# Causal attention in chunks of 512 queries and steps of four heads instead of head by head

## The chip, the cores and the metric

The program runs on one core of a Trainium2 chip. Its five engines (PE is TensorE, DVE is VectorE, ACT is ScalarE, POOL is GpSimd, SP only issues DMAs) run instruction streams of their own and meet at semaphores. The metric is the time of one execution on the device in microseconds. Before the change three runs took 2035.68 to 2046.28, median 2041.61.

## The reference, cut to what matters

A batch of one, 2048 tokens of width 128, goes through eight layers: Mamba with a feed-forward, a mixture of experts, attention, the mixture again, a second Mamba, a low-rank MLP, attention with ALiBi, the MLP again. Only the two attentions are changed. Each is, after one or two layer norms,

```python
q, k, v = split(x @ W)                    # 16 heads of 8
s = q @ k.T                               # (q is scaled by 8 ** -0.5)
s = s + slope[head] * (key - query)       # the second attention only (ALiBi)
s = where(key > query, -inf, s)           # causal
x = x + softmax(s) @ v @ W_out
```

It is to be exact to about float32, so q and k are each split into three bfloat16 parts, and a score is one matmul over 72 rows (3 x 3 x 8; 84 with ALiBi).

## The kernel before, in words

The function is `attention`, called twice (tags a0 and a1). Tokens fall into 16 tiles of 128 and into four chunks of 512 (`NC`). All of it goes by score tiles, of which a head has 40, in two forms:

- **q-items** (`item`, L1641 and L1807) compute scores with queries on partitions, in a tile of 128 queries by up to 512 keys, only to find each query's maximum. PE writes four groups of 32 rows into a PSUM bank of `ps_q` (three banks), and DVE reduces it (L1817) or, on the diagonal, masks and reduces it (L1814).
- **k-items** (`scores`, L1658) compute the scores again with keys on partitions, 128 keys by up to 512 queries, with three more rows that subtract the maxima. ACT takes the exponential (L1757) into `probs`, and `times_v` (L1675) multiplies four items at a time by v in float32, with a column of ones that gives the sums. The four 32-row groups of PE work side by side into `ps_o`; ACT copies the result of a chunk to `o_sb` (L1763).

Between them stand the maxima of a head: DVE negates them (L1822), POOL splits them into three bfloat16 parts (`split_maxima`, L1892), PE turns them (`turn`, L1632), DVE copies them out (L1805) and SP moves them by DMA into the operand (`load_maxima`, L1961). The k-items of the head wait for that.

The order is by head: head 0's 40 q-items, then 14 more (`LEAD`), and from then on one q-item per k-item. Inside a head chunk follows chunk, each with more keys (4, 8, 12 and 16 items). On PE, `scores` runs three items ahead of `times_v`; the streams of all engines are in order.

Operands: the parts of q and k go chunk by chunk to DRAM (`store_parts`, L1936), since each of their rows has to be repeated, and come back as `q_op` and `k_op` with 2048 columns, one pair per head, four pairs in turn (`load`, L1957; two DMAs, four with ALiBi). POOL copies v of a head next to the ones (`place`, L1887). SP's order in a head: stores of `o_sb` (`store`, L1966, four DMAs per chunk to DRAM), the maxima of the next head, the outputs of the head before back from DRAM with heads on partitions (`load_output`, L1972), the operands four heads on.

The output can only be made when all heads are there. For each chunk: DVE adds the four row groups of the sums and inverts them (`invert`), PE spreads them over the partitions (`spread`, L1692), DVE and POOL add the four groups of the outputs (`add_partials`, L1835, POOL's half L1931), DVE divides, PE multiplies by W_out (`output`), DVE adds to x and begins the next layer norm. Chunks 0 and 1 have their PE parts placed inside the last head's stream (L1730 to L1738); chunks 2 and 3 follow it. These parts use two PSUM tensors of their own, in the place of the projections'.

## Time and profile before

| | |
|---|---|
| median of 3 runs | 2041.61 us |
| the profiled execution | 2046.62 us |
| its span, first to last instruction | 2044.8 us |
| busy in the span | PE 89%, DVE 78%, ACT 57%, POOL 27% |
| mean granted TensorE clock | 0.943 |
| first attention | 508.0 to 986.0 us |
| second attention | about 1508 to 1985 us |

Busy shares are means over layers of quite different kinds, so they say little of the attentions: a stretch of the trace, cut out by its times, says more. "Granted clock" is the share of full speed that the TensorE throttle gave, 1.0 for 2.4 GHz and 0.5 for 1.2 GHz. A row of a timeline has the start in microseconds from the span's start, the duration, the engine, the line, what is written and read, how many instructions are merged (x), and in brackets the idle time of the engine before it and what ended that. SPq and ACTq rows are DMA issues; their duration is the issue's, not the transfer's.

### The profile page before, as it was taken

What the parts mean: (1) busy time and instruction counts of PE and PEld (TensorE: products, weight loads), DVE (VectorE), ACT (ScalarE), POOL (GpSimd) and SP (SyncE); (2) the same over time, 40 slices, a digit from 0 to 9 for tenths busy, and PEclk for the clock granted to TensorE, in tenths of its full rate; (3) what the DMA queues carried; (4) which work ended last, traced back from release to release, by engine and by line L of the source; (5) the groups of instructions that cost most, each with busy time, mean ns of one, the idle gap of its engine ahead of it and who ended that gap; (6) DMA issues with size and microseconds to landing.
All of it is one profiled execution on the core that took longest, in us unless ns stands there. A gap on an engine that the chain in (4) does not pass through costs nothing. (4 is left out here: it accounts for less than half of the span.)

```text
span 2044.8 us, 47996 instructions
## 1 busy us (share of the span) xinstructions
PE 1824.5 (89%) x18588; PEld 980.9 (48%) x18588; DVE 1587.9 (78%) x3383; ACT 1174.7 (57%) x2361; POOL 555.7 (27%) x520
## 2 busy tenths in 40 slices
PE   6888888999799999997899978888869999999967
PEld 2444454444255555554544434443634555555454
DVE  7899965666889999983465579999668999999545
ACT  4775623122278888885322256765443888888815
POOL 3898920000200000001000049988230000000022
PEclk9999998999699999998799989999886999999969
DMA  5343300310312222211041114443021233322200
GB/s 169 122 134 123 119 1 4 87 51 27 109 34 54 55 52 51 49 27 22 1 84 51 31 58 119 129 119 103 1 73 51 54 56 60 57 57 41 31 4 21
DMA packets 68527, 127.30 MB, mean 62 GB/s; under 512 B 20679, under 2 KB 30932, under 8 KB 66828
## 3 DMA queue, kind: packets, MB, share of 16 engines
q1 hardware_dynamic: 67884, 123.70, 24.2%
q8 instruction: 147, 2.41, 0.5%
q14 instruction: 80, 0.66, 0.1%
q10 hardware_dynamic: 416, 0.54, 0.1%
HBM read 105.58 MB, written 16.84 MB: 60 GB/s over the span
## 5 line engine op out<-in xcount | busy, mean ns | idle before, releaser
L1757 ACT ACTIVATE a_probs<-a_ps_k 128x512 f32<-128x512 f32 (+3 forms) x1280 | 598.6, 547 | 225.6 <-PE a_ps_k L1671 129.7
L1653 PE MATMUL a_ps_q<-a_k_op,a_q_op 84*32 84x512 bf16 (+7 forms) x5120 | 536.3, 366 | 25.4 <-DMA a_k_op<-a_k_parts 10.1
L1817 DVE TENSOR_REDUCE a_maxes<-a_ps_q 128x1 f32<-128x512 f32 x768 | 504.2, 686 | 67.8 <-PE a_ps_q L1653 65.2
L1667 PE MATMUL a_ps_k<-a_q_op,a_k_op 87*32 87x512 bf16 (+7 forms) x5120 | 517.8, 353 | 2.4 <-ACT a_probs L1757 0.8
L1689 PE MATMUL a_ps_o<-a_probs,a_vh 128*32 128x512 f32 (+3 forms) x2752 | 319.2, 509 | 0.8 <-ACT a_probs L1757 0.8
L1653 PEld LDWEIGHTS a_ps_q<-a_k_op,a_q_op 72*32 72x32 bf16 (+1 forms) x5120 | 186.9, 97 | 172.2 <-DVE a_maxes L1817 69.2
L1814 DVE CUSTOM_DVE_ANT_0 a_ps_q<-a_ps_q,all_c_mask_q 128x128 f32<-128x128 f32 (+3 forms) x512 | 248.2, 496 | 4.7 <-PE a_ps_q L1653 3.7
L1667 PEld LDWEIGHTS a_ps_k<-a_q_op,a_k_op 75*32 75x32 bf16 (+1 forms) x5120 | 184.9, 96 | 136.2 <-ACT a_probs L1757 85.6
L1088 ACT ACTIVATE e_silu<-e_psg,all_me_b 128x512 f32<-128x512 f32 x128 | 87.7, 687 | 229.0 <-PE e_psg L1020 228.9
L1897 POOL CAST a_max_parts<-a_neg_max 128x16 bf16<-128x16 f32 x32 | 6.3, 197 | 751.5 <-DVE a_neg_max L1822 751.5
L1171 DVE SCALAR_TENSOR_TENSOR e_mid<-e_psv,all_me_b,e_silu 128x512 f32<-128x512 f32 x128 | 95.7, 749 | 132.0 <-PE e_psv L1022 128.0
L172 POOL TENSOR_TENSOR all_rstd<-all_var_eps,all_c_minus_half 128x4 f32<-128x4 f32 x36 | 36.8, 1023 | 504.4 <-DVE all_var_eps L161 504.4
L662 POOL TENSOR_TENSOR m0st_read<-m0st_state,m0st_c_rows 128x1024 f32<-128x1024 f32 x64 | 149.6, 2358 | 12.4 <-DVE m0st_state L590 6.4
L590 DVE TENSOR_TENSOR_SCAN m0st_state<-m0st_decay,m0st_carry,m0st_drive 128x1024 f32<-128x1024 f32 x64 | 146.8, 2334 | 7.6 <-DVE m0st_drive L570 6.4
L590 DVE TENSOR_TENSOR_SCAN m1st_state<-m1st_decay,m1st_carry,m1st_drive 128x1024 f32<-128x1024 f32 x64 | 146.8, 2334 | 7.2 <-DVE m1st_drive L570 6.1
L662 POOL TENSOR_TENSOR m1st_read<-m1st_state,m1st_c_rows 128x1024 f32<-128x1024 f32 x64 | 149.5, 2357 | 9.9 <-PE m1st_psy L414 5.8
L1671 PE MATMUL a_ps_k<-all_c_mask_k,all_c_ident_b 128*32 128x128 bf16 x2048 | 149.3, 221 | 0.7 <-issue 0.7
L1020 PE MATMUL e_psg<-e_xT,all_me_w_T 128*128 128x512 f32 x256 | 134.7, 608 | 1.5 <-ACT e_xT L197 1.5
L1022 PE MATMUL e_psv<-e_xT,all_me_w_T 128*128 128x512 f32 x256 | 133.2, 602 | 0.0
L1009 PE MATMUL e_pso<-e_hid,all_me_w_T 128*128 128x512 f32 x256 | 119.0, 594 | 5.0 <-DVE e_hid L1180 5.0
L1689 PEld LDWEIGHTS a_ps_o<-a_probs,a_vh 128*32 128x32 f32 x2752 | 106.7, 110 | 26.7 <-issue 2.1
L414 PE MATMUL m0st_psy<-m0st_read,all_c_ident 128*128 128x512 f32 x256 | 115.8, 594 | 1.9 <-POOL m0st_read L662 1.8
(295 smaller groups left out, 2582.8 us busy)
## 6 DMA issues: line engine op xcount, KB each, us to landing
m0st_c_rows<-m_bc_rows SPq DMA_DIRECT2D x32, 512.0 KB
e_w_rows<-e_comb SPq DMA_DIRECT2D x64, 256.0 KB, 3.2
m1st_c_rows<-m_bc_rows SPq DMA_DIRECT2D x32, 512.0 KB
a_q_op<-a_q_parts SPq DMA_DIRECT2D x30, 288.0 KB
a_k_op<-a_k_parts SPq DMA_DIRECT2D x30, 288.0 KB
a_outputs<-a_o_sb SPq DMA_DIRECT2D x480, 18.0 KB
m0st_b_rows<-m_bc_rows SPq DMA_DIRECT2D x32, 256.0 KB
m1st_b_rows<-m_bc_rows SPq DMA_DIRECT2D x32, 256.0 KB
```

Source lines behind the costliest of these rows:

```text
L590: dve.tensor_tensor_scan(state[half(q, h)][:, :], decay[half(q, h)][:, :], drive[:, h, :], carry[:, h, q % NS:q % NS + 1], ALU.mult, ALU.a ...
L662: pool.tensor_tensor(read[h][:, :], state[half(q, h)][:, :], c_rows[q % 2][:, :], ALU.mult).then_inc(read_ready, 1)
L1009: pe.matmul(pso[:, :], w["w3_T"][:, e, f, :], hid[:, k % SL, :], start=k == 0, stop=k == K - 1, skip_group_check=True).then_inc(hid_free, 1)
L1020: pe.matmul(psg[:, f, :], w["w1_T"][:, e, fs], xT[:, tokens(c)], start=True, stop=True).then_inc(g_ready, 1)
L1022: pe.matmul(psv[:, f, :], w["w2_T"][:, e, fs], xT[:, tokens(c)], start=True, stop=True).then_inc(v_ready, 1)
L1653: last = pe.matmul(ps_q[32 * r:32 * r + 32, use % QB, 0:width], q_op[h % SLOT][0:NR, part(t, r)], k_op[h % SLOT][0:NR, kc * CH:kc * CH + w ...
L1667: last = pe.matmul(ps_k[32 * r:32 * r + 32, b % KB, 0:width], k_op[h % SLOT][:, part(j, r)], q_op[h % SLOT][:, c * CH + first:c * CH + fir ...
L1671: last = pe.matmul(ps_k[32 * r:32 * r + 32, b % KB, 0:P], g["ident_b"][:, part(0, r)], g["mask_k"][:, :], start=False, stop=True, skip_gro ...
L1689: pe.matmul(ps_o[rows, c % 2, lo:hi], vh[h % SLOT][:, j, :], probs[:, a % PSLOT, lo - first:hi - first], start=j < 4, stop=j >= TPC * c, s ...
L1757: act.activation(probs[:, n % PSLOT, 0:width], ps_k[:, b % KB, 0:width], ACT.Exp).then_inc(exp_done, 1)
L1814: dve.tensor_tensor_reduce(bank, bank, g["mask_q"][:, CH - width:CH], 1.0, -3e38, ALU.add, ALU.max, found).then_inc(q_read, 1)
L1817: dve.tensor_reduce(found, bank, AX.X, ALU.max).then_inc(q_read, 1)
```

## The change

The loops are turned round. A step is now one chunk of queries for four heads, and a call has 16 steps: chunk 0 for heads 0 to 3, 4 to 7, 8 to 11, 12 to 15, then chunk 1, and so on. A step of chunk 0 has 16 items, of chunk 1 32, of chunk 2 48, of chunk 3 64. The number and the shapes of all items stay as they were.

- q-items run one step and 14 items ahead (`position`): while a step's k-items run, the q-items of the next step are spread evenly over them, two per k-item in step 3, 1.5 in step 7, 1.33 in step 11.
- Maxima are turned per step (16 columns, as before per head).
- `q_op` holds a step (four buffers); keys are kept in `k_op`, one tensor per chunk, for all heads, and are loaded once. SP issues for each step, three steps on, one DMA for q and one for k per head, eight in all (nine with ALiBi), with 512 columns each instead of 2048.
- v stands in one tensor `vh` with the ones beside it, written by the projections; POOL's copy per head goes.
- A store moves two heads, and is issued twice a step. A chunk's outputs come back in five DMAs (chunk 3's by step, the last step's straight from `o_sb`).
- The outputs of chunks 0 to 2 are made inside the stream of the next chunk, at fixed positions (`prepare_at` to `normalise_at`); PE's parts use banks of `ps_q`. POOL adds sums and outputs there (`add_partials`); for chunk 3 DVE does most of it.
- Operands now share memory with the parts, so exponentials begin after all parts are stored.

The core of the diff:

```diff
+        HG = 4
+        GROUPS = HEADS // HG
+        STEPS = NC * GROUPS
+        turn_at = {begin[s + 1] + TURN: s for s in range(STEPS)}
+        POSITIONS = NI + TURN + 1
+        def position(b):
+            s, i = k_items[b][0], b - begin[k_items[b][0]]
+            after = size[s + 1] if s < LAST else size[s]
+            return min(begin[s + 1] + LEAD + -(-(i + 1) * after // size[s]), POSITIONS)
+        def event(c, n):
+            return position(begin[GROUPS * (c + 1)] + n)
+        prepare_at = {event(c, 24): c for c in range(NC - 1)}
+        spread_at = {event(c, 34): c for c in range(NC - 1)}
+        output_at = {event(c, 42): c for c in range(NC - 1)}
+        stats_at = {event(c, 46): c for c in range(NC - 1)}
+        normalise_at = {event(c, 60): c for c in range(NC - 1)}
...
@@ tensor
+            for b in range(NI):
+                if b + KB < NI:
+                    scores(b + KB)
+                first_forms(done, position(b))
+                done = position(b)
+                if b % 4 == 3:
+                    times_v(b - 3)
+            spread(NC - 1)
+            output(NC - 1)
...
@@ scalar
+            for c in range(1, NC):
+                act.wait_ge(stored[c], STORED)
...
@@ gpsimd
+            def add_partials(c):
+                add_sums(c)
+                add_upper(c)
+                if c:
+                    pool.wait_ge(q_ready, output_use[c - 1] + 1)
+                pool.tensor_tensor(total[:, :], oT[:, 0, :], oT[:, 1, :], ALU.add).then_inc(lower_ready, 1)
+                pool.wait_ge(lower_ready, c + 1)
+                pool.wait_ge(upper_ready, c + 1)
+                pool.tensor_tensor(total[:, :], total[:, :], upper[:, :], ALU.add).then_inc(total_ready, 1)
+            for s in range(STEPS):
+                c = chunk_of(s) - 1
+                if c > 0 and s % GROUPS == 1:
+                    add_partials(c)
+                split_maxima(s)
+                if c >= 0 and s % GROUPS == 1:
+                    if c == 0:
+                        add_partials(c)
+                    ahead.power(pool, c)
...
@@ sync
+            def load(s):
+                c, h = chunk_of(s), head(s, 0)
+                if s % GROUPS == 0:
+                    sp.wait_ge(stored[c], STORED)
+                if s >= SLOT:
+                    sp.wait_ge(k_ready, begin[s - SLOT + 1])
+                for hh in range(HG):
+                    loaded = step_loaded[s % SLOT] if s else first_head[hh]
+                    q_rows = q_dram[c, h + hh, :, :, :].rearrange("a d t -> (a d) t").unsqueeze(1)
+                    sp.dma_start(q_op[s % SLOT][0:PAIRS, hh * CH:(hh + 1) * CH],
+                                 q_rows.broadcast_to([SPL * DH, SPL, CH])).then_inc(loaded, 16)
+                    parts_k = k_dram[c, h + hh:h + hh + 1, :, :, :].rearrange("o d b t -> o (d b) t")
+                    sp.dma_start(k_op[c][0:PAIRS, (h + hh) * CH:(h + hh + 1) * CH],
+                                 parts_k.broadcast_to([SPL, DH * SPL, CH])).then_inc(loaded, 16)
...
+            load_k_rows(0)
+            store_parts(0)
+            for s in range(SLOT - 1):
+                load(s)
+                store_parts(s + 1)
+            for c in range(1, NC - 1):
+                load_k_rows(c)
+            load_maxima(0)
+            for c in range(1, NC):
+                sp.wait_ge(stored[c], STORED)
+            for s in range(STEPS):
+                c = chunk_of(s)
+                if s:
+                    store(s - 1, 1)
+                if s + SLOT - 1 < STEPS:
+                    load(s + SLOT - 1)
+                if s == GROUPS:
+                    load_k_rows(NC - 1)
+                if c == 0:
+                    load_maxima(s + 1)
+                if c and s % GROUPS == 0:
+                    load_outputs(c - 1, s - 1, 0, HEADS)
+                if c == NC - 1 and s % GROUPS:
+                    load_outputs(c, s - 1, head(s - 1, 0), HG)
+                if s < LAST:
+                    store(s, 0)
+                    if c:
+                        load_maxima(s + 1)
+            for hh in range(HG):
+                sp.wait_ge(o_read, HG * LAST + hh + 1)
+                if hh < HG - 1:
+                    move_sums(sp, hh)
+                move_outputs(sp, hh)
```

## Rows read from the trace of the kernel before

**Rows 1.** Busy time by stretch (from:to, length, busy us and count per engine).

```profile
core 0: us, PE busy (x) PEld busy (x) DVE busy (x) ACT busy (x) POOL busy (x), PEclk, DMA share, GB/s
508.00:559.30 51.30, 39.34 (x294) 15.10 (x298) 43.58 (x121) 12.85 (x22) 12.46 (x24) 0.69 0.36 109
602.30:626.70 24.40, 24.16 (x485) 14.19 (x475) 22.45 (x59) 20.22 (x45) 1.04 (x5) 1.00 0.29 52
928.00:944.50 16.50, 15.21 (x245) 6.07 (x237) 0.00 (x0) 15.86 (x36) 0.00 (x0) 1.00 0.33 43
944.50:963.60 19.10, 13.19 (x110) 8.40 (x111) 8.34 (x22) 4.09 (x9) 3.98 (x3) 0.73 0.05 8
963.60:986.00 22.40, 13.44 (x66) 11.88 (x66) 14.09 (x46) 0.60 (x1) 5.25 (x4) 0.59 0.02 3
```

**Rows 2.** Waits between 920 and 965 (total us, times, longest).

```profile
DVE a0ou_pair L1827 <- DMA a_sums<-a_outputs: 21.4, 1, 21.4
PE a0ou_ps_s L1697 <- DVE a0ou_inv L1833: 6.0, 2, 5.0
```

**Rows 3.** Timeline of PE in a head's middle (start, duration, ...).

```profile
583.54 1.03 PE L1689 MATMUL a_ps_o<-a_probs,a_vh 128*32 128x512 f32 x8
584.40 0.23 PE L1667 MATMUL a_ps_k<-a_q_op,a_k_op 75*32 75x128 bf16 x4
584.46 0.23 PE L1671 MATMUL a_ps_k<-all_c_mask_k,all_c_ident_b 128*32 128x128 bf16 x4
584.52 0.39 PE L1653 MATMUL a_ps_q<-a_k_op,a_q_op 72*32 72x512 bf16 x4
584.74 0.39 PE L1667 MATMUL a_ps_k<-a_q_op,a_k_op 75*32 75x512 bf16 x4
```

**Rows 4.** Timeline of DVE there.

```profile
582.60 0.69 DVE L1817 TENSOR_REDUCE a_maxes<-a_ps_q 128x1 f32<-128x512 f32 x1 [0.64 <-PE a_ps_q L1653]
583.21 0.42 DVE L1814 CUSTOM_DVE_ANT_0 a_ps_q<-a_ps_q,all_c_mask_q 128x256 f32<-128x256 f32 x1
583.55 0.68 DVE L1817 TENSOR_REDUCE a_maxes<-a_ps_q 128x1 f32<-128x512 f32 x1
```

**Rows 5.** DMA issues of SP in the timeline, and one line's durations (ns).

```profile
517.33 0.58 SPq L1942 DMA_DIRECT2D a_k_parts<-a0pr_k_parts  x1
...
522.15 0.90 SPq L1949 DMA_DIRECT2D a_q_op<-a_q_parts  x1
...
535.09 0.78 SPq L1949 DMA_DIRECT2D a_q_op<-a_q_parts  x1
535.91 0.71 SPq L1950 DMA_DIRECT2D a_k_op<-a_k_parts  x1
...
581.72 0.76 SPq L1963 DMA_DIRECT2D a_q_op<-a_max_T  x1
...
938.93 1.33 SPq L1979 DMA_DIRECT2D a_sums<-a_outputs  x4
...
L1970 SPq DMA_DIRECT2D a_outputs<-a_o_sb x480: 264/315/2105, 566.1 to 1930.1; - x160
```

**Rows 6.** Timeline of ACT in the last head.

```profile
936.65 3.27 ACT L1757 ACTIVATE a_probs<-a_ps_k 128x512 f32<-128x512 f32 x7
```

**Rows 7.** Timeline of the call's end, PE and ACT's DMA queue.

```profile
960.98 2.00 PE L1697 MATMUL a0ou_ps_s<-a0ou_inv,all_c_sel_head 128*128 128x64 f32 x16 [0.97 <-DVE a0ou_inv L1833]
...
964.37 1.16 PE L1705 MATMUL a0ou_ps_y<-all_a_wo,a0ou_total 128*128 128x128 f32 x8
...
965.25 3.60 ACTq L1605 DMA_DIRECT2D a_sums<-a_o_sb  x4
```

**Rows 8.** Timeline of the adds, DVE and POOL.

```profile
946.67 1.36 POOL L1931 TENSOR_TENSOR a0ou_upper<-a_oT 128x512 f32<-128x512 f32 x1 [22.56 <-DMA a_sums<-a_outputs]
946.95 1.17 DVE L1831 TENSOR_TENSOR a0ou_inv<-a0ou_pair 128x64 f32<-128x64 f32 x1
...
967.88 0.22 DVE L1831 TENSOR_TENSOR a0ou_inv<-a0ou_pair 128x64 f32<-128x64 f32 x1
```

More of the change, by code:

```diff
@@ L1464, in attention @@
         QB = 3
+        PB = 3
         LEAD = 14
         TURN = 5
[L1467 removed]
+        THIRD = 6
         JT = CH // SB
@@ L1583, in attention @@
-        USES = len(item_use) + len(turn_use)
-        def stream(turn, item, first, last):
-            for p in range(first, min(last, POSITIONS)):
-                if turned_at(p) is not None:
-                    turn(turned_at(p))
-                if p < NQ * HEADS:
-                    item(p // NQ, p % NQ)
-        def pieces(n):
-            c, j, first, width = k_items[n]
+        LOADS = 16 * (2 * HG + (1 if alibi else 0))
+        KROWS = [16 * (3 if alibi else 1)] + [16 * (2 if alibi else 1)] * (NC - 1)
@@ L1595, in pieces, with chunk_of, head @@
+        spread_use[NC - 1], output_use[NC - 1] = uses, uses + 1
+        def chunk_of(s):
+            return s // GROUPS
+        def head(s, hh):
+            return HG * (s % GROUPS) + hh
+        def pieces(b):
+            s, hh, j, first, width = k_items[b]
+            c = chunk_of(s)
             if c and j == TPC * c:
@@ L1656, in item, with spread @@
                 last.then_inc(q_ready, 1)
-            def scores(b):
-                h, n = divmod(b, NK)
-                c, j, first, width = k_items[n]
-                if n == 0:
-                    pe.wait_ge(max_loaded[h % SLOT], 16 * (h // SLOT + 1))
+            def spread(c):
+                use = spread_use[c]
+                pe.wait_ge(inverted, c + 1)
+                bank_free(use)
+                for j in range(SB):
+                    last = pe.matmul(ps_q[:, use % QB, j * JT:(j + 1) * JT], g["sel_head"][:, j, :], inv[:, :], start=True, stop=True)
+                last.then_inc(q_ready, 1)
@@ new lines, in output, with first_forms @@
+            def output(c):
+                use = output_use[c]
+                pe.wait_ge(q_read, spread_use[c] + 1)
+                bank_free(use)
+                for j in range(TPC):
+                    last = pe.matmul(ps_q[:, use % QB, tile(j)], total[:, tile(j)], w["wo"][:, :], start=True, stop=True)
+                last.then_inc(q_ready, 1)
+            def first_forms(begins, stops):
+                for p in range(begins, stops):
+                    if p in turn_at:
+                        turn(turn_at[p])
+                    if p in spread_at:
+                        spread(spread_at[p])
+                    if p in output_at:
+                        output(output_at[p])
+                    if p < NI:
+                        item(p)
@@ L1714, in _ @@
             pe.wait_ge(max_set, 3)
-            stream(turn, item, 0, NQ + LEAD)
-            pe.wait_ge(ones_loaded, 16 * SLOT)
+            pe.wait_ge(norm.copied, NC)
+            for bank in range(2):
+                for r in range(4):
+                    pe.matmul(ps_o[32 * r:32 * r + 32, bank, :], zeros[:, :], g["sel"][:, 0:4, :], start=True, stop=True,
+                              skip_group_check=True)
+            first_forms(0, begin[1] + LEAD)
             pe.wait_ge(v_copied, NC)
+            pe.wait_ge(v_set, 1)
             for o in range(2):
@@ L1721, in _ @@
                 scores(b)
[L1722 to L1741 removed]
+            done = begin[1] + LEAD
+            for b in range(NI):
[7 more added lines that the diff above has]
+            output(NC - 1)
         @block.scalar
@@ L1867, in _ @@
                 remove_first(c)
-            third_of_k(NC - 1)
             dve.wait_ge(max_set, 3)
-            stream(turn, item, 0, POSITIONS)
-            dve.wait_ge(k_ready, NK * LAST)
-            dve.wait_ge(o_back, 16 * BACKS * LAST)
-            for c in range(NC):
-                invert(c)
-                add_partials(c)
-                divide(c)
-                if c:
-                    ahead.normalise(dve, c - 1)
-                add(c)
-                if c + 1 < NC:
-                    dve.wait_ge(added, c + 1)
-                    ahead.stats(dve, c)
+            for p in range(POSITIONS):
+                if p == THIRD:
+                    third_of_k(NC - 1)
+                if p in prepare_at:
+                    invert(prepare_at[p])
+                if p in turn_at:
+                    turn(turn_at[p])
+                if p in spread_at:
+                    divide(spread_at[p])
+                if p in output_at:
+                    add(output_at[p])
+                if p in stats_at:
+                    ahead.stats(dve, stats_at[p])
+                if p in normalise_at:
+                    ahead.normalise(dve, normalise_at[p])
+                if p < NI:
+                    item(p)
```

507 lines of the change are left out of this document (220 added, 287 removed).

## The prediction

> **What bounds the kernel now.** I read the page's slices first: the two attention calls fill slices 11 to 19 and 31 to 39 of 40, with TensorE at nine tenths in most. Both run the changed function, so the case is this function, twice. I then cut the first call (508.0 to 986.0) into stretches [rows 1]. Until 559.3, the first exponential, the projections and the first 54 q-items run, at a granted clock of 0.69. One head in the middle takes 24.40 us with PE busy 24.16, DVE 22.45 and ACT 20.22, at full clock. From 928.0 the last head's k-items run alone, ACT busy 15.86 of 16.50. From 944.5 to 963.6 PE, ACT and DVE are all partly empty; from 963.6 to 986.0 chunks 2 and 3 of the output are made one after the other. So PE bounds the body with DVE close behind, and the edges cost 51.3 us ahead of the first exponential and 22.4 behind the last.
>
> The waits of the tail [rows 2] name the hole before 963.6: DVE waits 21.4 us for `a_sums`, and PE for `a_inv`. PE's stream asks for the sums of chunks 0 and 1 in the middle of the last head, before they are back. The 9 tiles left at 944.5 take 19 us where ACT needs about 0.5 each: some 14.5 us are lost.
>
> **Durations.** Four 32-row matmuls of 512 columns hold PE 0.22, of 128 columns or masks 0.06 (by their starts, [rows 3]), so a thousand columns cost 0.42 us at full clock. P times V of four full tiles holds it 0.86; for four diagonal tiles I take 0.64 by their 384 columns, and 0.85 plus 0.16 of zero fills in chunk 0. A reduce holds DVE 0.60, a masked reduce of 256 columns 0.34 [rows 4]; 128, 384 and 512 then take 0.21, 0.47 and 0.60, together 1.62. PE per head and chunk: chunk 0 2.29, chunk 1 (7168 columns, PV 1.49) 4.48, chunk 2 7.04, chunk 3 9.6; sum 23.4 against 24.40 measured. I put 3% on top, not the measured 4%, since long and short tiles stand less unevenly beside each other. A step of four heads: 9.4, 18.5, 29.0, 39.7. DVE for a step's q-items, with 0.5 for turn and negation: 7.3 in chunk 0 (diagonal tiles alone follow one another more slowly), then 16.6, 26.2, 35.8.
>
> **Ahead of the first exponential.** Before, the first load was issued at 522.15, behind the parts of chunk 1 [rows 5]. Now it goes right behind the parts of chunk 0, at about 521, so the first q-item comes 2 us earlier. But SP now issues eight loads a step: 0.78 and 0.71 with gaps, 1.58 a head, 6.35 a step [rows 5]. Its order is load 0, parts 1 (four DMAs near 0.6, 2.4), load 1, parts 2, load 2, parts 3, then the maxima: 521 + 3 x (6.35 + 2.4) + 0.6 + 0.76 = 548.6, landed 2.3 later. (The maxima issued at 581.72 for 0.76 served scores at 584.74 [rows 5, 3]: 2.3 is an upper end.) Only 30 narrow q-items are needed first, not 54, and they are done by about 545: SP ends this stretch. First exponential at 551.5 instead of 559.3: 7.8 gained. Ends: 10 if landings are quicker, 5 if they are as slow as that of the parts (issued 517.33, used by 522.15).
>
> **Steps 0 to 2.** Here I expect the largest loss in the body. In a short step SP issues, in this order, the second store (it waits for the fourth head's output of the step before), eight loads, the maxima. Queued behind its wait are the loads and the maxima; for the maxima PE's scores of the next step wait, and behind those PE's q-items too, as its queue is in order, and then DVE. From the first scores of a step: last PV and copy with hand-overs 3.3, four stores of 0.32 [rows 5] 1.3, loads 6.35, maxima 0.76, landing 2.3: 14.0 us, against 9.4 of PE work. Step 0 starts at the lower clock and takes 10, its maxima being ahead. So 10 + 14 + 14 = 38. Ends: 30 if everything of SP is hidden, 46 if PE works at 1.2 GHz besides.
>
> **The body.** The q-items run one step ahead and so meet a longer step at 3, 7 and 11, where DVE bounds: 16.6, 26.2, 35.8, not PE's 13, 22, 32.5. There the maxima also have fewer positions in which to land (nine at up to double rate, less three tiles): 1.6 + 0.9 + 0.5. Steps 4 to 6: 55.5; 8 to 10: 87.0; 12 to 14: 119.1 less 1.9 for 13 tiles without q-items. Step 15 is ACT's: seven full tiles take 3.27 [rows 6], a diagonal group 1.41 and a copy 0.47 by the same rate, so 12 x 0.477 + 1.41 + 0.47 = 7.6 a head, 30.4. Three tiles at the seam add 1.8, the end takes 1.3 off: 1.8 + 16.6 + 3.0 + 55.5 + 26.2 + 87.0 + 35.8 + 117.2 + 30.4 - 1.3 = 372.2.
>
> The outputs of chunks 0 to 2 now stand in this stream: spread 2.00 and product 1.16 on PE [rows 7], 3 x 3.16 = 9.5. On DVE some 4.4 a chunk are added: the 14.09 it had for two chunks and the end of a third [rows 1] make 6, less the adds that go to GpSimd. PE and DVE overlap but for 0.3 a chunk: 10.5. Ends: 3 if they fall in gaps, 15 if they never overlap. DVE's reciprocal waits for sums that went to DRAM and back and for GpSimd's two adds; its divide for three more, 1.36 each beside work [rows 8]; every q-item of DVE is queued behind, and PE waits for DVE to free a bank. The chunk's loads are issued 12 to 15 us into the step, the waits stand at 17 and 23. I take 4 us in all; ends 0 and 15. Sum: 38 + 372.2 + 10.5 + 4 = 424.7, against 404.3 from 559.3 to 963.6 before: 20.4 lost, although the 14.5 us hole is gone. What takes them: 78 tiles at the end without q-items instead of 54, DVE-bound seams, outputs in the stream, SP.
>
> GpSimd's adds beside DVE have a price in the trace: DVE's two-input add for `a_inv` took 1.17 beside GpSimd's `a_upper`, 0.22 alone [rows 8]. A q-item reads at most its mask from SBUF, and 22.45 of 24.40 us of DVE are q-items; I price nothing, the end is 5 us a chunk if they block each other throughout. The Trainium skill (SBUF — State Buffer, "Who interferes with whom") says that DVE with two SBUF inputs contends with GpSimd's reads, a reduce never. By that rule the price is 0; the row agrees for the two-input case.
>
> **The end.** Only chunk 3 is left. From the last exponential: PV and copy to 965.25 1.7, four DMAs on ACT's queue 3.60 [rows 7], landing 2.2, sums and reciprocal 1.2, spread 4.0 and product 2.3 at the lower clock (twice rows 7), divide and add 1.5: 16.5 instead of 22.4, so 5.9 gained. Ends 3 and 9.
>
> **Sum.** Per call -7.8 + 20.4 - 5.9 = +6.7, twice +13.4 (the second call's slices look the same). The profiled execution took 2046.6 (span 2044.8), 5 above the median of 2041.6; 13.4 on the median gives **2055**.
>
> **Rivals.** (1) Not slower: the even mix hides more. A head of 24.40 holds 23.4 of columns. If the long steps run 1% above their columns, outputs fall in gaps, round trips are early and SP's chain is 2 us shorter in each of two steps, a call loses 5 + 7 + 4 + 4 = 20 less: 2055 - 40 = 2015. For it: in a head where PE bounds, DVE still idles 0.64 at a time before a reduce [rows 4], so imbalance costs. Against: PE is 99% busy. It decides once a step of chunk 3 takes under 39 us and steps 1 and 2 under 12. (2) Clock: SP's holes of 4.6 us leave PE idle, and over the hole before 963.6 the granted clock was 0.73 [rows 1]. PE's work of steps 0 to 3 at 1.2 GHz is 2 x (3 x 9.4 + 13) = 82 instead of 54.6: +27 a call, 2109; half of it 2082. The Trainium skill (TensorE: Matmul & The Clock Gate, "HAM oscillation — how this bites in real kernels") tells of kernels that pay this at each DMA wait; the trace agrees in so far as the clock fell at the hole. (3) The sums' round trip: issued by 940.26, used at 946.67 [rows 5, 8], 6.4 us. Then each of three chunks waits 5 us at reciprocal and divide: +11 a call, 2077. (4) The hole only moves: the last chunk's own sums are as late, 22.4 stays behind the last exponential: 2067.
>
> **Chances.** Forecast 0.50 (own range 2040 to 2068), rival 1 0.22, rival 2 0.11, rivals 3 and 4 0.17. "No change" is within 0.5%, 10 us, about what a measurement of this kernel can tell. Faster 0.24 (rival 1 and an edge of the forecast), same 0.28 (the forecast's lower half), slower 0.48. The range leaves out half of rival 1 and half of rival 2: 2022 to 2084.
>
> **What would show it.** First exponential 43 to 44 us into a call; steps 1 and 2 near 14 us each, PE idle for the maxima's DMA while SP issues without a gap; DVE over 95% busy in steps 3, 7 and 11; the last step ACT-bound near 30; 16.5 us behind the last exponential. The forecast is wrong if the maxima never hold PE up, if a long step takes under 39 us, or if DVE waits 5 us or more for sums.

## The result, and the profile after

The changed kernel takes 2123.36 us (median of 4 runs, 2118.36 to 2128.21), the kernel before 2042.97 beside it: a ratio of 1.0396, 95% interval 1.0368 to 1.0423. It is 80 us slower where 13 were forecast, and outside the range. The profiled execution took 2124.45, its span is 2122.4.

The first call now runs from 508.0 to 1023.9, 37.9 us longer; the second is 44.3 longer, and the rest of the program is 4.6 shorter between the two profiles. The loss stands between the first and the last exponential of a call: 451.6 and 452.2 us where it was 404.3 and 403.0. Behind the last exponential 15.4 and 15.6 are left of 22.4 and 23.8. Cut at the first exponential of each step, as [rows 1] were cut (from:to, length, busy us by engine, granted clock, DMA share, GB/s), the page after reads:

```profile
508.00:556.90 48.90, 26.53 (x218) 13.22 (x218) 28.52 (x103) 12.74 (x22) 10.40 (x15) 0.69 0.37 112
568.60:583.60 15.00, 9.24 (x229) 7.52 (x224) 8.16 (x36) 7.81 (x21) 0.80 (x4) 0.93 0.27 66
583.60:599.80 16.20, 12.35 (x246) 10.00 (x242) 9.15 (x28) 8.14 (x21) 0.80 (x4) 0.82 0.24 57
599.80:619.70 19.90, 16.62 (x290) 11.15 (x286) 16.36 (x46) 8.72 (x20) 0.80 (x4) 0.86 0.18 44
619.70:644.70 25.00, 20.47 (x415) 11.78 (x411) 19.61 (x55) 16.46 (x36) 2.87 (x8) 0.96 0.38 91
644.70:670.30 25.60, 24.86 (x426) 13.81 (x422) 20.18 (x61) 16.79 (x36) 4.29 (x7) 0.90 0.16 38
670.30:690.20 19.90, 19.55 (x400) 11.23 (x394) 18.96 (x53) 16.38 (x36) 0.80 (x4) 1.00 0.20 48
690.20:717.20 27.00, 25.04 (x458) 11.12 (x454) 26.36 (x66) 17.05 (x36) 0.80 (x4) 1.00 0.15 36
782.00:811.70 29.70, 29.49 (x562) 16.68 (x558) 27.51 (x66) 24.34 (x53) 0.80 (x4) 1.00 0.14 33
811.70:849.80 38.10, 36.33 (x618) 14.98 (x614) 36.46 (x82) 25.68 (x52) 0.80 (x4) 1.00 0.11 26
849.80:895.60 45.80, 44.41 (x750) 22.74 (x746) 40.36 (x96) 33.33 (x69) 6.32 (x10) 1.00 0.21 48
895.60:936.40 40.80, 40.52 (x722) 20.08 (x718) 38.09 (x87) 32.91 (x69) 0.80 (x4) 1.00 0.08 17
974.90:1008.50 33.60, 31.15 (x452) 10.91 (x448) 0.00 (x0) 31.70 (x69) 0.00 (x0) 1.00 0.10 21
1008.50:1023.90 15.40, 6.59 (x34) 5.57 (x34) 4.22 (x7) 0.60 (x1) 1.26 (x1) 0.60 0.03 6
```

These are steps 1 to 7, 10 to 13 and 15 between the prelude and the end; 8, 9 and 14 took 33.8, 31.0 and 38.5, step 0 11.7. PE's work is unchanged, so read length against PE busy first: steps 1 to 4 have 3 to 6 us without PE. Then read the clock: it is under 1.00 in the same steps and in 5. There PE is busy 24.86 us against 19.55 in step 6; some 3.2 of the difference are the output's spread and product [rows 7], and at full clock the same step took 23.1 instead of 25.6 (experiment 4). From step 6 on the clock is full; long beside their neighbours are the steps with an output (8, 9, 12), those whose q-items are of the next chunk (7, 11) and ACT's last step.

The waits of PE over the whole program (total, times, longest) name what ends the holes; in the kernel before PE never waited for the maxima's DMA in its first call:

```profile
PE a_ps_k L1723 <- DMA a_q_op<-a_max_T: 50.1, 12, 13.8
PE a_ps_q L1689 <- DVE a_inv L1869: 14.6, 2, 7.3
```

One hole closely, first SP's queue in step 1 (four stores, four pairs of loads of which the last stands here, the maxima), then PE's timeline, then the stretch of the hole and the one behind it:

```profile
570.98 1.36 SPq L2031 DMA_DIRECT2D a_outputs<-a_o_sb  x4
572.44 0.81 SPq L2013 DMA_DIRECT2D a_q_op<-a_q_parts  x1
...
578.04 0.71 SPq L2016 DMA_DIRECT2D a_k_op<-a_k_parts  x1
578.79 0.73 SPq L2024 DMA_DIRECT2D a_q_op<-a_max_T  x1
```

```profile
582.84 0.62 PE L1723 MATMUL a_ps_k<-a_q_op,a_k_op 75*32 75x512 bf16 x4 [5.44 <-DMA a_q_op<-a_max_T]
```

```profile
577.40:582.80 5.40, 0.00 (x1) 0.00 (x0) 0.62 (x2) 0.77 (x2) 0.00 (x0) 0.87 0.34 94
582.80:588.20 5.40, 5.36 (x81) 4.16 (x85) 2.12 (x8) 2.49 (x6) 0.00 (x0) 0.50 0.02 4
```

SP issues without a gap and reaches the maxima at 578.79, just as forecast; they land 3.3 us after their issue ends, not 2.3 (in the second call it is 2.4 here and 2.1 a step later). And when PE comes back its clock is 0.50, half of 2.4 GHz. The Trainium skill (TensorE: Matmul & The Clock Gate, "HAM oscillation — how this bites in real kernels") describes this pair, a wait for a DMA and then work at half clock, once per wait; the trace agrees three times in the first call.

Step 4 shows the same with another transfer ahead. The last output step's traffic on SP (sums, the 1 MB of partial outputs, stores, maxima), and the answer on PE:

```profile
632.42 3.37 SPq L2042 DMA_DIRECT2D a_sums<-a_outputs  x4
635.83 0.60 SPq L2044 DMA_DIRECT2D a_oT<-a_outputs  x1
636.48 1.87 SPq L2031 DMA_DIRECT2D a_outputs<-a_o_sb  x4
638.39 0.80 SPq L2024 DMA_DIRECT2D a_q_op<-a_max_T  x1
...
644.05 0.62 PE L1723 MATMUL a_ps_k<-a_q_op,a_k_op 75*32 75x512 bf16 x4 [3.96 <-DMA a_q_op<-a_max_T]
```

Here landing takes 4.9 us. In the second call the same step fails in another way: the sums come late, GpSimd adds them late, DVE waits to invert, and PE behind it (DVE's timeline and the waits of 1675 to 1683):

```profile
1679.86 0.55 DVE L1869 RECIPROCAL a_inv<-a_inv 128x64 f32<-128x64 f32 x1 [4.56 <-POOL a_inv L1949]
...
PE a_ps_q L1680 <- DVE a_maxes L1856: 4.4, 1, 4.4
```

### The profile page after: what moved, and what is told of

Same layout as the page of the kernel before. It is cut to its first block and busy times, and to the rows that moved or that the text cites. A ratio compares the mean times of both kernels' runs of the same rounds, so it can differ in the third digit from the quotient of the medians.

```text
span 2122.4 us, 47829 instructions
## 1 busy us (share of the span) xinstructions
PE 1839.6 (87%) x18604; PEld 955.4 (45%) x18604; DVE 1579.5 (74%) x3359; ACT 1185.8 (56%) x2361; POOL 562.0 (26%) x498
## 5 line engine op out<-in xcount | busy, mean ns | idle before, releaser
L1792 ACT ACTIVATE a_probs<-a_ps_k 128x512 f32<-128x512 f32 (+3 forms) x1280 | 608.3, 544 | 247.2 <-PE a_ps_k L1727 139.2
L1723 PE MATMUL a_ps_k<-a_q_op,a_k_op 75*32 75x512 bf16 (+7 forms) x5120 | 536.3, 357 | 57.7 <-DMA a_q_op<-a_max_T 50.1
L1680 PE MATMUL a_ps_q<-a_k_op,a_q_op 72*32 72x512 bf16 (+7 forms) x5120 | 527.9, 363 | 45.9 <-DVE a_maxes L1856 13.8
L1745 PE MATMUL a_ps_o<-a_probs,a_vh 128*9 128x512 f32 (+3 forms) x2752 | 322.4, 511 | 0.9 <-ACT a_probs L1792 0.9
L1727 PE MATMUL a_ps_k<-all_c_mask_k,all_c_ident_b 128*32 128x128 bf16 x2048 | 162.1, 227 | 0.0
L414 PE MATMUL m1st_psy<-m1st_read,all_c_ident 128*128 128x512 f32 x256 | 116.1, 594 | 2.0 <-POOL m1st_read L662 1.7
```

What stands on the lines that cost most here:

```text
L414: last = pe.matmul(psy[:, h, chunk(b)], g["ident"][:, :], read[h][:, chunk(b)], start=False, stop=q % NS == NS - 1, skip_group_check=True)
L1680: last = pe.matmul(ps_q[32 * r:32 * r + 32, use % QB, 0:width], q_op[s % SLOT][0:NR, tokens:tokens + 32], k_op[kc][0:NR, h * CH:h * CH + w ...
L1723: last = pe.matmul(ps_k[32 * r:32 * r + 32, b % KB, 0:width], k_op[j // TPC][:, keys:keys + 32], q_op[s % SLOT][:, hh * CH + first:hh * CH ...
L1727: last = pe.matmul(ps_k[32 * r:32 * r + 32, b % KB, 0:P], g["ident_b"][:, 32 * r:32 * r + 32], g["mask_k"][:, :], start=False, stop=True, ...
L1745: pe.matmul(ps_o[32 * r:32 * r + DH + 1, bank, lo:hi], vh[:, HEADS * j + h, :], probs[:, a % PSLOT, lo - first:hi - first], start=j < 4, s ...
L1792: act.activation(probs[:, b % PSLOT, 0:width], ps_k[:, b % KB, 0:width], ACT.Exp).then_inc(exp_done, 1)
```

## The experiments

Theories: **T1**, the maxima's way through SP's queue (issue order, landing behind other DMAs, half clock behind each hole); **T2**, the outputs of chunks 0 to 2 inside the stream; **T3**, the step structure itself, where it loads DVE. Gains below are differences between the changed kernel's ratio, 1.0396, and the ratio of the experiment, each with the kernel before beside it, times 2040 us; by the two intervals such a gain is known to 6 to 10 us. "Body" below is the stretch from the first to the last exponential of a call in the profiled execution, 451.6 and 452.2 us in the kernel after; it leaves out what varies in the other layers.

**1. Maxima ahead of the loads.**

```diff
-                load(s + 3); load_maxima(s + 1)        # step order of SP
+                store(s, 0); load_maxima(s + 1); load(s + 3)
```

> SP issues the next step's maxima ahead of the loads of the step after the next three (and load 2 of the prelude behind the first maxima); nothing else changes. Theory T1 (most of the 80 us is PE waiting for the maxima, 50.1 us in the trace after, because SP issues them behind eight loads of 0.7 to 0.8 us and they land behind these, and because PE's clock is half for 6.8 us after each hole): first exponential 4 to 5 us earlier in each call, steps 1, 2, 4 and 5 together 11 us shorter, a few us elsewhere; the waits for the maxima fall from 50.1 to under 15 us and the time to 2085 (2078 to 2095). Theory T2 (the outputs of chunks 0 to 2 in the stream cost 5 us each and more): this order changes little, the maxima wait moves behind another, 2110 to 2123. Theory T3 (the steps themselves are longer: seams where DVE bounds, a longer end without q-items): holes go, but PE then waits for DVE instead, at least 2110.

Measured 2117.56, ratio 1.0385 (1.0354 to 1.0416): 2 us, no gain beyond the noise and far from the 38 that T1 expected. The first exponential stands at 545.9 instead of 556.9, but in this profile the call itself begins 4.1 us earlier: it came 6.9 us sooner, 7.5 in the second call. Against that steps 1 and 2 grew to 18.5 and 20.1, and the body was 453.0 and 455.8. Waits of PE from 508 to 617:

```profile
PE a_ps_q L1680 <- DMA a_k_op<-a_k_parts: 16.4, 5, 6.7
PE a_ps_k L1723 <- DMA a_q_op<-a_max_T: 10.9, 5, 2.7
```

The wait moved: q-items run 30 items ahead of their k-items in steps of 16, so the loads are as urgent as the maxima, and one queue cannot put both first. T1's remedy failed, not yet T1. With nothing ahead of them the maxima landed 1.51 to 1.56 us after their issue ended (eight times).

**2. The maxima on GpSimd's queue**, SP's order as in the kernel after.

```diff
                 split_maxima(s)
+                pool.wait_ge(q_read, turn_use[s] + 1)
+                pool.dma_start(q_op[s % SLOT][NR:NR_MAX, :]..., max_T[:, :]).then_inc(max_loaded[s % SLOT], 16)
```

> SP's order stays as in the kernel after, but the maxima go out on GpSimd's own queue as soon as DVE has copied them. T1 in its form that SP's order and queue hold the maxima back: the holes of 5.44, 3.78 and 3.96 us shrink to under 1.5, 2085 (2078 to 2095), as with the other order. T1 in its form that the transfers of the loads fill the DMA engines whatever the queue: the maxima are issued 3 to 9 us earlier but take 5 to 6 us to land, so about half is gained: 2100 to 2112. T2 or T3: 2110 to 2123. The prelude's hole of 9.46 us should go to 4 or less in the first form, as there the maxima could be issued at about 543 instead of 547.94.

Measured 2101.79, ratio 1.0314 (1.0290 to 1.0337): 17 us. Steps 1 and 2 (and step 3):

```profile
559.60:569.00 9.40, 9.08 (x246) 7.93 (x240) 8.07 (x36) 7.63 (x21) 1.41 (x5) 1.00 0.27 62
569.00:580.10 11.10, 9.76 (x244) 8.01 (x236) 8.87 (x29) 7.82 (x22) 1.41 (x5) 1.00 0.36 94
580.10:599.00 18.90, 14.08 (x290) 9.00 (x281) 16.04 (x47) 8.38 (x22) 1.41 (x5) 1.00 0.27 66
```

Step 1 at 9.40 is the columns' own 9.4: SP's queue was the loss there, 10.7 us in two steps of the first call. Little of that is left at the end: the body is only 2.2 and 2.9 us shorter, since steps 4, 5, 7, 8 and 11 lose some 10 us in the first call (8 alone 3.8), and most of the gain is the stretch ahead of the first exponential, 5.2 and 8.4 us. With the 1 MB in flight the maxima took 5.4 us on this queue too (issued 618.86, 0.62, used 624.92), and steps 4 and 5 were 54.4 instead of 50.6. So both forms of T1 hold: order where loads are ahead, traffic on the shared DMA engines where the 1 MB is.

**3. Two loads a step instead of eight**, the same bytes.

```diff
-                for hh in range(HG): sp.dma_start(q_op[...hh...], ...); sp.dma_start(k_op[c][...hh...], ...)
+                sp.dma_start(q_op[s % SLOT][0:PAIRS, :], ...four heads); sp.dma_start(k_op[c][...h:h + HG...], ...)
```

> The kernel after with SP's order, but the operands of a step come in two DMAs of four heads each instead of eight of one head; the same bytes (the parts of k are stored in three DMAs instead of one a chunk, which adds two issues of 0.5 to 0.6 us to each of four chunks ahead of the first exponential). T1a (SP's issue time holds the maxima back: 8 x 0.78 = 6.3 us a step): a step's chain is some 4.5 us shorter, steps 1 and 2 fall from 15.0 and 16.2 to about 11, the hole of 9.46 before the first exponential shrinks by 2 to 5 us, 2 x 14 less: 2095 (2085 to 2102). T1b (the transfers themselves, 0.6 MB a step in the same queue, hold them back): landing stays 2.7 to 4.9 us behind the issue and the holes stay, 2112 or more. The other queue gained 5.6 and 5.2 us in steps 1 and 2 by taking away both.

Measured 2106.49, ratio 1.0334 (1.0312 to 1.0356): 13 us, between the two. A load of four heads is issued as quickly as one of one head:

```profile
568.40 0.81 SPq L2020 DMA_DIRECT2D a_q_op<-a_q_parts  x1
569.25 0.72 SPq L2023 DMA_DIRECT2D a_k_op<-a_k_parts  x1
570.10 0.73 SPq L2031 DMA_DIRECT2D a_q_op<-a_max_T  x1
...
577.06 0.62 PE L1723 MATMUL a_ps_k<-a_q_op,a_k_op 75*32 75x512 bf16 x4 [3.69 <-DMA a_q_op<-a_max_T]
```

From the step's first exponential (564.6) the maxima are issued after 5.5 us instead of 10.2, but land 6.2 us later: the bytes queued ahead come first. Of 4.7 us saved at the issue 1.8 reach the step (13.2 instead of 15.0). Steps 4 and 5 of the first call gained more, 22.5 and 23.1 at a clock of 1.00: the sums and the 1 MB go out earlier too.

**4. PE kept busy through the holes**, to price the clock alone. PE's wait for a free bank of `ps_k` moves ahead of the fill with it.

```diff
+                    for n in range(FILL.get(s, 0)):      # {2: 18, 3: 14, 4: 6, 5: 14}
+                        pe.matmul(ps_k[:, b % KB, :], g["ident_b"][0:96, :], g["sel"][0:96, 0:4, :], start=True, stop=True)
                     pe.wait_ge(max_loaded[s % SLOT], ...)
```

> The kernel after with matmuls into a bank that is overwritten next, put on TensorE between the last work before a step and its wait for the maxima: 18, 14, 6 and 14 of 512 columns ahead of the scores of steps 2, 3, 4 and 5 (3.8, 2.9, 1.3 and 2.9 us at full clock). They shorten no wait. If the half clock behind each hole (6.8 us each at 581.4, 598.4, 642.8 in the first call, four stretches in the second) is an own cost on top of the hole, the clock stays at 1.0 there, the steps behind run 2 to 3.4 us shorter each: 15 to 20 us over both calls, 2105. If PE is not what bounds the short steps behind a hole (SP's chain is), nothing comes of it: 2118 to 2125. Where a hole is shorter than its matmuls, up to 2 us is lost.

Measured 2118.69, ratio 1.0394 (1.0367 to 1.0421): no difference. In the first call it did what it should: clock 1.00 in steps 1 to 4, which with step 5 took 94.5 us instead of 101.7.

```profile
568.80:583.40 14.60, 12.94 (x248) 9.03 (x245) 8.10 (x35) 7.77 (x22) 0.80 (x4) 1.00 0.26 66
583.40:598.00 14.60, 12.86 (x260) 9.51 (x256) 8.90 (x28) 7.75 (x20) 0.80 (x4) 1.00 0.26 64
```

In the second call, which among steps 1 to 5 had the full clock in step 1 only, step 4 ran into the wait for the sums instead (5.1 us, then 13.7 us at half clock) and took 32.2 instead of 27.8. So the half clock is a cost of its own, some 7 us in the first call, but this fill does not save it on the whole.

**5. No outputs of chunks 0 to 2.** Left out: their sums, divide, product, normalisation and loads.

```diff
-        prepare_at = {event(c, 24): c for c in range(NC - 1)}     # and spread_at, output_at, stats_at, normalise_at
+        prepare_at = {}
```

> Leaves out the output projection of chunks 0 to 2 with their sums, normalisation and the loads of their partial outputs; only chunk 3 gets its output. T2: the trace after shows steps 8 and 12 at 33.8 and 45.8 us against 29.7 and 40.8 without an output, and 25.0 for step 4, so some 5 us go from each of three chunks, 32 us over both calls, and with the 1 MB load gone ahead of the maxima in step 4 its hole of 3.96 us and the half clock behind it go too, 3 to 5 us a call: 2123 - 40 = 2083. T1: only the hole of step 4 goes, the rest of the outputs lies in gaps: 2110 to 2116. The waits for the maxima stay above 35 us in both.

Measured 2081.64, ratio 1.0218 (1.0197 to 1.0240): 36 us, T2 as expected. The body says more, 428.2 and 429.7: 23 us a call. Steps 4, 5, 8 and 12 without an output, against 25.00, 25.60, 33.80 and 45.80:

```profile
615.80:637.50 21.70, 21.32 (x415) 12.67 (x411) 18.88 (x54) 16.46 (x36) 0.80 (x4) 0.92 0.21 51
637.50:656.40 18.90, 18.83 (x402) 10.70 (x397) 17.70 (x51) 16.35 (x36) 0.80 (x4) 1.00 0.21 51
702.70:732.50 29.80, 29.66 (x562) 15.77 (x558) 27.61 (x68) 24.38 (x52) 0.80 (x4) 1.00 0.14 33
829.90:870.20 40.30, 40.23 (x726) 21.48 (x722) 37.47 (x84) 32.98 (x68) 0.80 (x4) 1.00 0.10 25
```

**6. The engines' work of the outputs without the round trip.** The loads of partial outputs and sums of chunks 0 to 2 are left out; both buffers are set to one once.

```diff
-                if c and s % GROUPS == 0:
-                    load_outputs(c - 1, s - 1, 0, HEADS)
+                if s == 3: pool.memset(sums, 1.0); pool.memset(oT, 1.0)      # GpSimd, in its idle time
```

> The kernel after without the loads of the partial outputs and sums of chunks 0 to 2: GpSimd sets both buffers to one once (in step 2 or 3) and all adds, the reciprocal, divide, product and normalisation run on that, as often as before. Without outputs at all 42 us went. If the round trip is what costs (sums and 1 MB behind eight loads, the maxima behind the 1 MB: holes of 3.96 and 4.41 us with half clock behind them in steps 4 and 5), most of it goes in steps 4 and 5 and little in 8 and 12: 12 to 18 us over both calls, 2107 (2103 to 2112). If it were all round trip: 2085. If it is engines' work alone: 2118 or more. What stays of the 42 us is the work on PE and DVE, which the forecast put at 10.5 us a call.

Measured 2101.15, ratio 1.0302 (1.0285 to 1.0318): 19 of the 36 us, slightly more than expected. The body is 442.6 and 441.5, 9.0 and 10.7 shorter, more than half of it in steps 4 and 5 (21.8 and 23.2 in the first call, from 25.0 and 25.6; 20.3 and 23.2 in the second, from 27.8 and 25.2), and one us each in 8 and 12. Steps 4, 5 and 8 here:

```profile
619.60:641.40 21.80, 21.42 (x415) 12.84 (x407) 18.96 (x55) 16.46 (x37) 5.29 (x9) 0.92 0.20 50
641.40:664.60 23.20, 22.47 (x426) 13.06 (x422) 20.34 (x63) 16.43 (x36) 1.82 (x5) 1.00 0.18 42
711.40:744.10 32.70, 32.60 (x586) 18.53 (x582) 29.77 (x71) 24.41 (x52) 0.80 (x4) 1.00 0.12 30
```

What remains is the work on PE and DVE. By the ratios it is 17 us, 8.5 a call; the steps are the sharper reading. Step 5 takes 23.2 with the work and 18.9 without, 8 32.7 and 29.8, 12 44.8 and 40.3, steps 6, 9 and 13 some 3 us more together. The body of the first call is 14.4 us longer with the work than without (11.8 in the second), where the forecast had 10.5.

**7. Orders 1 and 5 together.**

> The order of the first kernel of this set and the outputs of chunks 0 to 2 left out. If the two causes are separate, the gains add but for the hole of step 4 that both take away: 2123 - 38 - 40 + 8 = 2053. What stands above the kernel before less its own hole is then T3's share: steps of chunk 2 at 29.7 and of chunk 3 at 40.8 us against 24.4 a head in the middle before (97.6 for four heads): 2045 to 2060. If T3 were small the time would be under 2035; if either gain only moves work to another wait, over 2075.

Measured 2086.15, ratio 1.0243 (1.0217 to 1.0269). A miss, and consistent with experiment 1: that order gains nothing, with outputs or without (steps 1 and 2: 19.3 and 20.5).

**8. Experiments 2 and 5 together.**

> The maxima on GpSimd's queue and the outputs of chunks 0 to 2 left out (only chunk 3 gets its output). The first gained 21 us alone, the second 42. In the first, steps 4 and 5 became longer (26.4 and 28.0 us against 25.0 and 25.6) and step 8 too (37.6 against 33.8): if that is the 1 MB load and GpSimd's adds in the way of the maxima, it goes with the outputs: 2123 - 42 - 35 = 2046 to 2052, and what is left over the body of the kernel before is the step structure (T3). If the longer steps are GpSimd's queue itself (slow issue, waits of GpSimd for DVE), the gains only add: 2060 to 2064. T3's own account: steps 0 to 15 then sum to 404 us, as 404.3 before with a hole of 14.5 in it.

Measured 2048.10, ratio 1.0047 (1.0030 to 1.0064): 71 us, more than the sum of the two, 17 and 36, so the maxima and the 1 MB do hurt each other. The body is 420.9 in both calls. The account of T3 in that text was added up wrongly: the steps sum to 420.9 us, not 404.

**9. Half of DVE's reducing**, in the kernel after and in the kernel before. Left out: the maxima of the second half of each q-item's columns; exponentials are scaled by 0.25.

```diff
+                    bank = bank[:, 0:width // 2]
```

> The kernel after, but DVE takes the maxima of the first half of each q-item's columns only (a scale of 0.25 in the exponential keeps it in range); PE, ACT and all transfers as before. If DVE bounds the steps whose q-items belong to the next, longer chunk (3, 7, 11: busy 16.4, 26.4, 36.5 of 19.9, 27.0, 38.1 us), these fall towards PE's work: 14, 23, 34, some 14 us a call, and the output steps by 1 to 2 each, so 2123 - 32 = 2091 (2084 to 2100). If they are long for the order in which PE meets long and short tiles, or for SP, under 3 us a call: 2117 or more.

> The same edit in the kernel before, to tell what DVE costs there: PE is busy 24.16 of 24.40 us a head, DVE 22.45. At most the 0.24 us a head and the start of the first head: 2041 - 8 = 2033 (2028 to 2040). If it gained as much as in the kernel after, DVE would not be what the change brought up.

Measured 2076.01, ratio 1.0177 (1.0145 to 1.0209), 45 us; and before 2022.95, ratio 0.9921 (0.9893 to 0.9948), 16 us. Both more than expected. Steps 3, 6, 7, 10 and 11 with DVE relieved:

```profile
598.70:615.00 16.30, 14.87 (x290) 10.27 (x286) 10.55 (x46) 8.34 (x20) 0.80 (x4) 0.90 0.22 54
663.20:681.80 18.60, 18.60 (x401) 12.24 (x395) 13.30 (x53) 16.27 (x37) 0.80 (x4) 1.00 0.21 51
681.80:704.40 22.60, 22.07 (x461) 13.36 (x457) 17.42 (x66) 16.71 (x37) 0.80 (x4) 1.00 0.17 43
767.00:796.00 29.00, 29.00 (x562) 18.08 (x558) 19.30 (x66) 24.24 (x53) 0.81 (x4) 1.00 0.14 33
796.00:829.00 33.00, 32.62 (x622) 17.93 (x617) 23.64 (x82) 25.32 (x53) 0.80 (x4) 1.00 0.13 30
```

18.6, 29.0 and, at the seams, 22.6 and 33.0 are the forecast's own figures for PE alone (18.5, 29.0, 22, 32.5). With DVE at its work the same steps take 19.9, 29.7, 27.0 and 38.1. DVE costs the changed kernel 29 us more than the one before, where a head fell from 24.4 to 23.9 only; three intervals stand behind the 29, some 10 us either way, and the bodies of both calls say 48 against 14.

**10. The outputs eight k-tiles later.**

```diff
-        prepare_at = {event(c, 24): ...}; spread 34, output 42, stats 46, normalise 60
+        prepare_at = {event(c, 32): ...}; spread 42, output 50, stats 53, normalise 68
```

> The kernel after with the outputs of chunks 0 to 2 put eight k-tiles later in the stream (reciprocal 32 instead of 24, divide 42 instead of 34, product 50 instead of 42, statistics 53, normalising 68). If the round trip of the sums and GpSimd's adds is what makes an output cost 5 us and more (in the trace after DVE waits 4.8 and 8.6 us for them and PE stands still 4.4 us in step 4 of the second call), 4 to 6 us a call go: 2113 (2108 to 2117). If the outputs cost what they hold PE and DVE (3.16 us of PE a chunk) or what their 1 MB load does to the maxima, which this edit leaves where it is, nothing changes: 2119 to 2126.

Measured 2136.09, ratio 1.0477 (1.0445 to 1.0509): 17 us slower, which neither side expected. The waits of 664 to 671 say why; GpSimd stands in the normalisation, and the next maxima are queued behind it:

```profile
POOL all_rstd L172 <- DVE all_var_eps L161: 21.4, 1, 21.4
PE a_ps_q L1661 <- POOL a_max_parts L1941: 3.4, 1, 3.4
```

**11. The remedies together**, nothing left out: the maxima on GpSimd's queue, load 2 behind the parts of chunk 3, partial outputs loaded ahead of the step's loads; first with the outputs eight tiles later, then without that.

> All that helped together, nothing left out: the maxima on GpSimd's queue, load 2 behind the parts of chunk 3, the load of the partial outputs ahead of the step's eight loads, the outputs eight k-tiles later. From the kernel with the maxima on GpSimd's queue (2102): the first exponential 2 to 3 us earlier, steps 4 and 5 from 54.4 to about 46 as without a hole behind the load, step 8 from 37.6 to 34: 14 us a call, 2102 - 28 = 2074 (2065 to 2085). It cannot reach the kernel before if the step structure costs some 30 us a call, as the kernel without outputs (first to last exponential 421 us against 385 before, for which its outputs stood outside) says.

> The maxima on GpSimd's queue, load 2 behind the parts of chunk 3, the load of the partial outputs ahead of the step's eight loads; the outputs where they stood in the kernel after. The kernel with these and the outputs eight k-tiles later took 2100.4; in its trace PE stands still 3.45 us in step 5 (647.24 to 650.69) for the turn of the next maxima, which GpSimd gives only behind the power of the normalisation, and half clock follows; step 9 has 32.6 us instead of 31.0. If this order is the cause, 6 to 8 us a call come back: 2100 - 14 = 2086 (2080 to 2092). If the load of the partial outputs ahead of the step's loads is what hurts: 2096 or more.

Measured 2100.38, ratio 1.0300 (1.0264 to 1.0336), against 2074 expected; and 2085.19, ratio 1.0218 (1.0179 to 1.0256), as expected. The difference is experiment 10's cause. The best version of the change gives back 36 of its 80 us and is still 45 slower than the kernel before.

**12. All three causes taken away** (experiments 2, 5 and 9).

> All three causes taken away: the maxima on GpSimd's queue, the outputs of chunks 0 to 2 left out, DVE's maxima over half of each q-item's columns. The first two gave 2048.1; DVE alone gave 47 of 2123 (2076.0), of which some is of the short steps' DVE time and not lost when there are no holes. If the causes add: 2048 - 40 = 2008 (2002 to 2014). If DVE's 47 us were partly the same waits as the outputs' (their DVE work in the same steps): 2048 - 30 = 2018. Over 2025 would say that something else is behind the remaining time.

Measured 2016.47, ratio 0.9885 (0.9868 to 0.9902): the second case, gains that overlap by some 12 us. The kernel before with the same relief of DVE has 0.9921, with all its outputs. With the outputs' work put back, 17 us by the ratios or 26 by the bodies, the changed kernel would stand at 0.997 to 1.001: some 10 to 20 us remain that no run names. The longer end without q-items may be the most of it (argued, not shown).

**13. The kernel before with two of SP's orders changed**, the only version with nothing left out that is under it.

```diff
-            for c in range(NC): store_parts(c); load_first(c - 1)    # last head: move_last(0), load_output(14)
+            for c in range(NC): store_parts(c); load_first(c)        # last head: load_output(14), move_last(0)
```

> The kernel before with two orders of SP changed: the partial outputs and sums of head 14 are loaded ahead of the moves of head 15 (issued at about 933 instead of 938.5), and the first head's operands of chunk c are loaded right behind the parts of chunk c instead of behind those of chunk c + 1. If the 21.4 us wait for the sums of head 14 sets the end, its hole of 14.5 us shrinks by 5 us in each call, and the first q-item comes 1 to 2 us earlier: 2041 - 13 = 2028 (2024 to 2032). If the moves of head 15 take the place of the sums as what comes last, or the first exponential waits for the last loads anyway: 2036 to 2042.

Measured 2035.43 against 2038.22, ratio 0.9984 (0.9972 to 0.9996): 3 us of the 13, within what was called no change. PE's wait of 5.02 us for the first inverse is gone, and the last head's stretch up to its last exponential took 27.4 us instead of 35.3 (27.0 instead of 34.9 in the second call), more than the 5 us expected. But the stretch ahead of the first exponential, where the other order was to gain 1 to 2 us, became 2.6 and 4.8 us longer. The two calls are 8.9 us shorter in the profiled execution, the fastest of 12. What DVE waits for at the end is now the last head's own sums, for 18.0 us instead of 21.4 [rows 2]:

```profile
DVE a0ou_pair L1827 <- DMA a_sums<-a_o_sb: 18.0, 1, 18.0
```

## Why the prediction was wrong

Its direction and its list of costs were right, its sizes not. First call, forecast against measured:

| stretch | forecast | measured | miss |
|---|---|---|---|
| to the first exponential | 43.5 | 48.9 | +5.4 |
| steps 0 to 2 | 38 | 42.9 | +4.9 |
| steps 3 and 7 with their seams | 47.1 | 46.9 | -0.2 |
| steps 4 to 6 with an output | 60.3 | 70.5 | +10.2 |
| steps 8 to 10 with an output | 91.8 | 94.5 | +2.7 |
| step 11 | 36.3 | 38.1 | +1.8 |
| steps 12 to 14 with an output | 122.1 | 125.1 | +3.0 |
| step 15 | 29.1 | 33.6 | +4.5 |
| the end | 16.5 | 15.4 | -1.1 |

(The 10.5 and 4 for outputs and sums are shared out evenly over the three chunks, and the 1.3 of the end stands in step 15. The 1.8 for three tiles at a seam stands with step 3, where the sum has it; counted with step 15, the misses of the two rows are +1.6 and +2.7.) The misses add to 31 us in the first call.

Experiments 5 and 6 split the body, forecast 424.7 and measured 451.6. Without the outputs it was 428.2 against a forecast of 410.2: 18.0 of the 31 are in the steps themselves. The outputs' work took 14.4 instead of 10.5, their round trip 9.0 instead of 4. So no single term failed; these did:

**The landing of the maxima**, "2.3 is an upper end", from one case with a quiet queue, is the mis-sized term of SP's chain. Issue times came true to 0.2 us (547.94 against 547.8), but landing took 1.5 us with nothing ahead, 2.1 to 3.3 behind loads, 4.9 to 5.4 with the 1 MB in flight, and 6.0 and 8.2 at the first exponential of the two calls. The DMA share in the holes is 0.34 to 0.64. In the first call this is 3.7 of the 5.4 us ahead of the first exponential, 1.0 in step 1 and 0.4 in step 2; in step 4 it made a hole that the forecast did not have. Most of what is left of the 5.4 is ACT's table load. In the kernel before it was done 17 us into the call; now it stands between the scores and the first exponential, and the forecast did not have it:

```profile
555.59 1.28 ACT L1792 ACT_TABLE_LOAD   x1 [30.13 <-PE a_ps_k L1727]
```

**The clock** was put at nothing in the sum and made a rival with 11%, as if holes of 4.6 us could come without it. They came together: experiment 4 puts it at 7 us in the first call. It also lengthens SP's chain. In step 2 the loads begin 5.6 us behind the first exponential (589.23), in step 1 3.8 (572.44), since the outputs whose stores stand ahead of them come later at half clock; with the clock full both steps took 14.6. That rival's other half, all short steps at 1.2 GHz, did not happen: step 1 has 0.93.

**The sums' round trip** was judged by its position in the stream (4 us). In steps 8 and 12 that held. In step 4 the loads of a step stand ahead of the sums on SP, whose issue takes 3.37 us for four DMAs of 32 KB, against 1.33 for four of 8 KB before [rows 5]. It is the 1 MB that makes the maxima late in the one call and the sums themselves in the other: 9 to 10.7 us a call by experiment 6, on top of 14.4 for the work. Rival 3 was right in kind, at one chunk of three and in one call of the two.

**PE at its columns plus 3%** (18.5, 29.0, 39.7) was right only where DVE does not interfere (experiment 9). DVE's share of the seams was well sized: 16.6, 26.2 and 35.8 forecast, 16.4, 26.4 and 36.5 busy in steps 3, 7 and 11. But a step in the middle of a chunk gives DVE more, 17.7, 27.6 and 37.5 in experiment 5, close to PE's own time, and such steps took 18.9, 29.8 and 40.3. That both engines near full cost more than the larger one was seen in the rows (DVE idle 0.64 before a reduce) and not priced. Steps 8 to 14 miss 7.5 us, 5.7 of them without outputs too.

**The last step** is ACT's, as forecast, but 31.70 us busy and 33.6 long instead of 30.4 less 1.3.

**Right:** the order of SP's queue and its times, SP as what ends the prelude, the seam of step 7 (27.0 against 27.1), the end (15.4, so rival 4 did not come), no loss from GpSimd's adds beside DVE: its 512-column reduce took 0.69 us beside one at 645.79 as without. Step 3 came out (19.9) by luck: DVE was busy 82% of it, not over 95, with a hole and half clock in it, and DVE relieved it still took 16.3 instead of PE's 13. Rival 1 was never near: a step of chunk 3 took 40.8, not under 39.

Not settled: why the half clock lasts longer in some holes, and how much of DVE's 29 us comes from the seams and how much from the even mix; by the steps of the first call about 13 and 11 of its 25 us, but with holes and clock mixed in.

## What to carry to other kernels

A small DMA on which the next stage waits gains from a queue of its own, which takes the order away but not the traffic, and its latency must be read where the DMAs are loaded: the same 12 KB took from 1.5 to 8.2 us. When a reordering makes stages short, list what must make a round trip within one stage, because each such trip that is late costs its hole and then a stretch at half clock. Before moving work into a stream where one engine is at 99%, look at the second busiest: it was DVE, at 92%, that made the longer steps expensive.

## What the runs showed of the hardware

- A broadcast load of four heads (2048 columns) is issued in 0.81 us like one of 512 columns (0.81), so joining DMAs saves issue time in full, but not the transfer.
- A DMA issued on GpSimd's queue held GpSimd 0.62 us, and in experiment 2 landed 1.5 to 3.6 us after its issue in seven waits without the 1 MB load, 5.4 with it, where SP's queue gave 1.5 with nothing ahead: steps 7 and 11 became 28.4 and 39.2 instead of 27.0 and 38.1.
- At each of six holes of 3.8 to 5.4 us in the kernel after PE's clock was 0.50 for 6.8 us, from within the hole into the work behind it; at one of 5.07 us (experiment 4, second call) for 13.7, with full work behind it.
